# A four-layer attention and feed-forward kernel: the first body's work in another order

## The reference

```python
x = x + L0_xattn(layernorm(x), ctx)   # 16 heads, softmax over 64 keys, then relu(out @ W1 + b1) @ W2 + b2
x = x + L0_ffn(layernorm(x))          # 8 experts, top 2, a shared wi/wo and a low-rank part per expert
x = x + L1_xattn(layernorm(x), ctx)   # one head of 256, keys and values from ctx
x = x + L1_ffn(layernorm(x))          # x @ weight.T + pooled x @ disha
```

## Time and profile before

| what | value |
|---|---|
| median of 3 runs | 320.92 us (320.5 to 321.01) |
| the profiled execution | 320.74 us |
| its span, first to last instruction | 318.7 us |
| so around the span | 2.0 us |
| granted TensorE clock, mean | 0.991 |
| TensorE busy | 97% of the span |
| VectorE, ScalarE, GpSimd busy | 75%, 53%, 51% |

### The profile page before, as it was taken

How to read it: one execution, slowest core, us unless ns; L and a number is a source line. 1 busy time by engine, 2 the same in 40 slices (tenths; PEclk the granted TensorE clock), 3 DMA queues, 4 the chain that set the end, 5 groups by cost and what they waited for, 6 DMA issues and landing times.

```text
span 318.7 us, 6483 instructions
## 1 busy us (share of the span) xinstructions
PE 307.6 (97%) x2485; PEld 282.8 (89%) x2485; DVE 237.8 (75%) x650; ACT 169.1 (53%) x345; POOL 161.3 (51%) x155
## 2 busy tenths in 40 slices
PE   8999999999999999999999999999999999999972
PEld 6778897999989998999999998999899989999961
DVE  4898775967896878877795789678868679455765
ACT  4347656673475357545746456635753574434520
POOL 1674773794065705572386308560557053803551
PEclk9999999999999999999999999999999999999996
DMA  8693430013010330215021400042012200000001
GB/s 246 189 408 123 135 100 2 0 43 106 19 11 10 81 118 2 16 44 140 20 16 26 140 35 17 2 99 101 3 15 51 82 4 0 2 33 2 0 33 34
DMA packets 15902, 20.02 MB, mean 63 GB/s; under 512 B 2912, under 2 KB 11872, under 8 KB 15616
## 3 DMA queue, kind: packets, MB, share of 16 engines
q1 hardware_dynamic: 14320, 16.57, 19.1%
q10 hardware_dynamic: 1552, 3.05, 2.7%
HBM read 11.48 MB, written 2.63 MB: 44 GB/s over the span
## 4 chain that ended last, share of the span: by engine, by line
PE 82%; DVE 6%; ACT 5%; DMA 3%; POOL 1%; issue 1%; ACTq 0%; POOLq 0%
PE psI L326 14%; PE psI L504 14%; PE psP L335 11%; PE psI L335 10%; PE psS L335 6%; PE psT L326 4%; DMA raw_w<-in_w 3%; PE psP L439 2%; PE psS L412 2%; PE psT L571 2%; PE psS L382 2%; PE psP L440 2%; PE psT L350 2%; PE psP L669 1%; PE psS L326 1%
## 5 line engine op out<-in xcount | busy, mean ns | idle before, releaser
L1570 POOL TENSOR_TENSOR rs<-ve,mhalf 128x2 f32<-128x2 f32 x30 | 21.9, 729 | 97.0 <-DVE ve L1166 97.0
L1589 POOL TENSOR_TENSOR hid_l<-r,hid_h 128x512 fp32r<-128x512 f32 x32 | 42.2, 1330 | 16.7 <-ACT hid_h L950 16.6
L945 ACT ACTIVATE r<-psI,first 128x256 f32<-128x256 f32 x60 | 25.1, 475 | 20.0 <-PE psI L504 20.0
L504 PE MATMUL psI<-at_h,lb_h 128*128 128x256 f32 x120 | 35.1, 292 | 0.0
L1259 DVE SCALAR_TENSOR_TENSOR r<-psI,nbi,r 128x256 f32<-128x256 f32 x60 | 26.1, 477 | 11.4 <-PE psI L504 11.4
L504 PE MATMUL psI<-at_l,lb_h 128*128 128x256 f32 x120 | 33.8, 282 | 0.0
L504 PE MATMUL psI<-at_h,lb_l 128*128 128x256 f32 x120 | 33.7, 281 | 0.0
L1583 POOL TENSOR_TENSOR hs_l<-hs,hs_h 128x512 fp32r<-128x512 f32 x16 | 21.0, 1312 | 21.7 <-ACT hs_h L930 20.9
L1200 DVE RECIPROCAL rec<-psP 128x256 f32<-128x256 f32 x16 | 28.0, 1752 | 1.2 <-PE psP L440 1.2
L876 ACT ACTIVATE xn<-xmid,nmr,rs 128x256 f32<-128x256 f32 x16 | 8.8, 594 | 38.0 <-POOL nmr L1574 38.0
L914 ACT ACTIVATE ex<-psS 128x512 f32<-128x512 f32 x30 | 17.1, 599 | 17.5 <-PE psS L412 15.8
(11 more groups left out here) (293 smaller groups left out, 877.2 us busy)
## 6 DMA issues: line engine op xcount, KB each, us to landing
stack<-qu_h SPq DMA_DIRECT2D x56, 64.0 KB, 2.0
xin<-in_x SPq DMA_DIRECT2D x8, 256.0 KB, 2.8
stack<-qu_l SPq DMA_DIRECT2D x28, 64.0 KB, 2.0
out<-x ACTq DMA_DIRECT2D x7, 256.0 KB, 2.0
xn<-in_xt SPq DMA_DIRECT2D x5, 256.0 KB, 2.9
raw_wi<-in_wi SPq DMA_DIRECT2D x1, 1024.0 KB, 7.4
raw_wo<-in_wo SPq DMA_DIRECT2D x1, 1024.0 KB, 11.0
kv<-in_kv SPq DMA_DIRECT2D x2, 384.0 KB, 6.3
```

Of the source, the lines that this page charges most:

```text
L504: last = mm(bank[:, k * T:(k + 1) * T], (WH, WL)[x]["lb"][:, 0, f * P:(f + 1) * P], AT[y][:, which, :], start=False, stop=q == 2, skip_gro ...
L945: last = A(R1[:, f, :], bank[:, k * T:(k + 1) * T], ACT.Relu, bias=cols[:, BI + f:BI + f + 1])
L1570: G_.tensor_tensor(rs[:, :], ve[:, :], mhalf[:, :], ALU.pow).then_inc(S(f"ln{j}_rs"), 1)
L1589: G_.tensor_tensor(HL[:, two, :], R1[:, two, :], as32(HH[:, two, :]), ALU.subtract).then_inc(S("hidl"), 1)
```

## The change

In the opening, `a_max_transposes(0)` moves from behind the second `opening_scores` to behind the first. The values of batch 1 move on TensorE from ahead of `a_scores` to behind them, on VectorE from ahead of block 1's statistics to behind `attended`. `query_means` moves from ahead of `a_attend` to behind `values1`. The transposes of block 1 move from ahead of `a_hidden(0, 0)` to behind it, and the three filler products go. On VectorE the copy to `wqm` and the `diagonal` products move from ahead of `xta_l` to behind it. ScalarE, GpSimd and SyncE keep their order.

```diff
@@ TensorE, body @@
                     if a == 0:
                         a_scores(a, 3)
-                        query_means()
+                        values(T_(1)[:, 0:D], kv0, 1).then_inc(S("v0_ps"), 1)
                     a_attend(a, 0)
...
                 if a == 0:
                     values1()
+                    query_means()
+                if A_:
+                    a_hidden(a, 0)
+                if a == 0:
                     pe.wait_ge(S("v0"), BATCH)
                     transposes(1, h, T_(1))
-                    filler(I_(0), 3)
-                if A_:
-                    a_hidden(a, 0)
@@ TensorE, opening @@
             opening_scores(0)
+            a_max_transposes(0)
             opening_scores(1)
-            a_max_transposes(0)
             opening_scores(2)
             opening_scores(3)
-            values(T_(1)[:, 0:D], kv0, 1).then_inc(S("v0_ps"), 1)
@@ VectorE, body @@
                 if a == 0:
-                    dve.wait_ge(S("centred"), 1)
-                    V.tensor_copy(wqm[:, :], T_(0)[:, D:2 * D]).then_inc(S("centred"), 1)
-                    diagonal(kd_h, kt0_h, "kd_h")
-                    diagonal(kd_l, kt0_l, "kd_l")
+                    first_values(1, T_(1)[:, 0:D])
...
                 if H_ and h < TURNED:
                     low(1, h, XTA, T_(1))
+                if a == 0:
+                    dve.wait_ge(S("centred"), 1)
+                    V.tensor_copy(wqm[:, :], T_(0)[:, D:2 * D]).then_inc(S("centred"), 1)
+                    diagonal(kd_h, kt0_h, "kd_h")
+                    diagonal(kd_l, kt0_l, "kd_l")
@@ VectorE, opening @@
             first_values(0, T_(0)[:, 0:D])
             low_weights("w1")
-            first_values(1, T_(1)[:, 0:D])
```

## The result

The changed kernel takes 323.54 us, the median of 4 runs (323.25 to 323.78), against 320.97 of the kernel before beside it (320.5 to 321.3): a ratio of 1.0073 with a 95% interval of 1.0051 to 1.0095. It is slower by 2.3 us by the ratio and by 2.6 us by the medians, and the predicted 323.5 holds. The profiled execution has 323.25 us and a span of 321.3.

A forecast was written before the change was run, and what follows sets the result against it. TensorE, busy 97%, bounds the kernel, with ScalarE full from 27 to 36.5 us; 1.65 us at hs_l plus 0.4 to 1.5 of standing gives 2.1 to 3.1, middle 2.6: 323.5 us, range 321.7 to 325.2.

The forecast's parts named there:

- The opening and VectorE: Opening up to oa_h: batch 1's values moved back gain 1.18 us; the earlier maxima gain VectorE nothing.
- The transposes: Block 1's transposes behind a_hidden(0, 0): xta_h at 28.38, ScalarE idle 2.2 us, the rest of its list 1.15 us later.
- The port: Diagonals meeting GpSimd's w_l: kd_l done at 33.6 or 34.7, products on hs_l at 37.0, 1.65 us later in all.
- The transfers: SyncE's queue from kd_l, 16.2 us: last landing at 49.8 to 50.9, TensorE standing 0.4 to 1.5 us at block 1's scores.
- The second, the clock: TensorE's new gaps at 25.5 and 31.1 us: clock falls to its lower level, 2 us more, 325.5; chance 0.10.
- the third, faster: Transposes don't hold ScalarE, given early xta_h or 2.2 us of slack before hs: gain 1.18 us stays, 319.7; chance 0.08.

The follow-up runs named there:

- e1: The changed kernel with the copy to wqm and the diagonals back ahead of xta_l; median 323.21 us, ratio 1.0073.
- e5: e1 with filler products on zeros in TensorE's two gaps, one ahead of the first hidden product, four behind block 1's queries; ratio 1.0037.
- e6: The changed kernel with the high parts of W2 and wi made on ScalarE ahead of block 1's normalisation; ratio 1.0066.
- e11: e7 with block 1's transposes where the change put them, behind the first hidden product; ratio 0.9974.
- e4: The changed kernel with eight high-query transfers of block 1 ahead of the key reads on SyncE's queue; ratio 1.0076.
- e9: The changed kernel with filler products on zeros in TensorE's two gaps, as in e5; ratio 1.0104.
- e10: e9 with the eight query transfers ahead of the key reads, as in e4; ratio 1.0072.
- e2: The changed kernel with block 1's transposes back ahead of the first hidden product, in bank I_(0); 320.8 us, ratio 0.9994.
- e12: e1 run once more for one trace; that execution took 323.95 us.
- e7: e3 with W2's and wi's high parts ahead of block 1's normalisation and W2's low part right behind block 1's scale on GpSimd; ratio 0.9963.
- e3: The changed kernel with both the transposes and the copy and diagonals back, the edits of e1 and e2 together; ratio 1.0016.

## Why the prediction was right

**The opening and VectorE.** 1.18 us were predicted up to oa_h; from the first row maximum it is 1.09. That the earlier maxima gain VectorE nothing came out for a reason a little different: GpSimd's ks waits for a VectorE operation that ended 1.1 us earlier in this execution, so ks was out of the way, and the mask L1505 waited for GpSimd's kb instead. It took 0.92 us where it takes 0.42 alone, and w_l started at 18.21, 0.05 later than before.

**The transposes.** ScalarE was predicted 1.15 us late with 2.2 us of idle time ahead of xta_h; the rows have 1.3 and 2.29. e1 and e5, which have this term alone, stand at +1.47 and +1.67 at L412; in their traces oa_h had gained 0.17 and 0.38 us less. e6 and e11 show the mechanism: with late transposes but without the weight parts behind xta_h, hs_l is ahead of the kernel before.

**The port.** The rows have one kd_h in ahead of w_l, the next held to 32.97, kd_l done at 33.64 (33.6 was one of the two ends) and hs_l's second operation stretched to 1.74. On TensorE's way it is worth 0.44 us: counted as in the table, the second hs_h is done 1.31 us later than before and the products on hs_l start 1.75 later. The same two places are 0.46 us apart in e4, e9 and e10 and 0.49 in e2, and not apart in e1 and e5, where the diagonals are back. The 0.5 predicted was right. (The totals of e1 and e10 against those of the changed kernel and e5 give only 0.27 and 0.25, because oa_h is not equally early in them.)

**The transfers.** Predicted 0.4 to 1.5 us of standing at L412, with the middle taken (by the prediction's own terms 0.3 to 1.4: 33.6 and 16.2 give 49.8, against TensorE's 49.5); measured 0.87 (+2.62 less +1.75), and 1.0 in time by e9 and e10. The end of kd_l was the early one, the chain behind it 0.4 us longer than before: two key reads took 2.10 instead of 1.27 us to issue, and one of the query transfers 0.4 less. With 16.2 us again, the wait would have been near the low end, so that the middle was met is luck.

**The sum.** ScalarE's term was 0.16 us low (1.15, measured 1.31), the port's 0.06 high (0.5, measured 0.44) and the transfers' 0.08 high (0.95, measured 0.87), so the mechanism and the sizes were right in the trace. That the median met 323.5 to 0.04 us is luck: medians and ratio give the loss as 2.6 and 2.3 us. The sizes of the single terms rest on one trace for each kernel. The timed ratios agree with them in the main and differ by up to 1.1 us, most for e1 and e3.

**The rivals.** The second, the clock, does happen: it is seen in the trace of e12, in the place named, at 0.65 us and not 2, and the mean clock of other executions of e1 and of the changed kernel points that way, though no trace shows where it fell in them. In the changed kernel itself the two executions with a mean near 0.983 took 0.2 us more than the other two, which is too few to tell. The ground given against this rival was weak: the clock was 0.99 between 310 and 313 us because it fell at 312.9, and between 311 and 314 it was 0.82, as the line under e7 shows. The stated condition of the third, faster, was wrong in part: e3 has ScalarE's gap undone and the gain does not stay, since the early W2 part meets the diagonals.

## What to carry to other kernels

An instruction that is moved takes its queue along: ask of each engine what stands behind it in the list (here 2.9 us of weight parts behind xta_h), what is started by its end on a slow path (16 us of transfers behind kd_l, with 2.5 us to spare), and what it will run beside. GpSimd's work is best placed beside VectorE's reads from PSUM, not beside its work on two operands in SBUF. A gain early in a chain is only real when nothing else in the chain was tied to the old time: e3 won 1.4 us at oa_h and kept none of it in time; e7, with W2's parts moved out of the way, is faster than the kernel before.

## What the runs showed of the hardware

VectorE work on two operands in SBUF and GpSimd work exclude each other, and the traces show it to a few hundredths of a us. A VectorE operation that was held up ends a fixed time after GpSimd's: 0.29 us for a 128x256 mask or kd part (18.00 to 18.29 and 32.68 to 32.97 in the changed kernel), 1.08 for a 128x1024 low part (31.35 to 32.43 before, 34.78 to 35.86 in the changed kernel). Between two VectorE instructions a waiting GpSimd one gets in (w_l between the two kd_h), and the other way round. A GpSimd operation on only 16 partitions (ks, 2.77 us) holds VectorE out as well: before, ks ended at 17.96 and the mask at 18.24. So does VectorE with a GpSimd operation on two numbers in each partition: nmr took 1.10 us in e2 instead of 0.20. The reciprocals, which read PSUM, don't take part: GpSimd's w_l took 2.35 us beside them.

In e12's trace TensorE's granted clock fell to its lower level (1.2 of 2.4 GHz) at 35.4 us, shortly behind the end of a gap of 2.04 us, and was back before 40 us. In e1's trace, the same kernel with a gap of 2.06 us in the same place, it did not fall. By the mean clock, six of this kernel's seven executions were like e12 (0.983 to 0.985), and none of the 12 of e5 with products on zeros in the gap (0.988 and above); where the clock fell in the other five, no trace shows. The Trainium skill (TensorE: Matmul & The Clock Gate, "HAM oscillation") advises against longer gaps only; by e12's trace a gap of 2 us is enough at times. The page and the trace differ here, and the trace decides.
